# Selective scan: summing the states' products in channel layout instead of in token rows

## Reference, cut to what matters

```python
deltaA = jnp.exp(delta[..., None] * A)                     # A has 16 states for each of 512 channels
deltaBx = (delta * xs)[..., None] * B[:, :, None, :]
_, ys = jax.lax.associative_scan(combine, (deltaA, deltaBx), axis=1)   # h[t] = deltaA*h[t-1] + deltaBx
y = jnp.einsum('blcn,bln->blc', ys, C)                     # y = sum over n of h_n * C_n
out = (y + xs * D) * res
return x + out @ w_out
```

## Time and profile before

| | |
|---|---|
| runs | 2469.58, 2472.93, 2481.07 us; median 2472.93 |
| the profiled execution | 2463.2 us, its span 2461.4 us |
| granted TensorE clock, mean | 0.954 |
| first scan, last scan (start) | 69.2 us, 2339.4 us |
| instructions | 35873 |
| moved by DMA | 101.76 MB, mean 41 GB/s |

### The profile page before, as it was taken

How to read it: one execution, slowest core, us unless ns; L and a number is a source line. 1 busy time by engine, 2 the same in 40 slices (tenths; PEclk the granted TensorE clock), 3 DMA queues, 4 the chain that set the end, 5 groups by cost and what they waited for, 6 DMA issues and landing times.

```text
span 2461.4 us, 35873 instructions
## 1 busy us (share of the span) xinstructions
PE 2128.8 (86%) x9268; PEld 1287.6 (52%) x9268; DVE 2187.0 (89%) x2820; ACT 1843.2 (75%) x3897; POOL 1854.4 (75%) x1324
## 2 busy tenths in 40 slices
PE   5687789898998989899898988989898998988797
PEld 2355455464655546465554646555464655546454
DVE  1889999998999999998999989999999989999931
ACT  6566787868788786978778687887869788785644
POOL 3868697887879788786877868797887879787620
PEclk8797899999999999999999999999999999999999
DMA  6011110111102021110202011020211102011100
GB/s 136 27 39 47 31 44 23 64 32 53 36 20 63 23 66 31 54 35 25 60 23 61 32 56 36 14 69 23 62 31 57 35 16 68 22 54 33 35 1 17
DMA packets 83404, 101.76 MB, mean 41 GB/s; under 512 B 23480, under 2 KB 49872, under 8 KB 83168
## 3 DMA queue, kind: packets, MB, share of 16 engines
q1 hardware_dynamic: 83168, 99.06, 13.7%
HBM read 90.13 MB, written 8.91 MB: 40 GB/s over the span
## 4 chain that ended last, share of the span: by engine, by line
PE 31%; DVE 28%; issue 21%; ACT 10%; POOL 8%; DVEq 1%; ACTq 0%; DMA 0%; POOLq 0%
PE bank L798 16%; DVE h L1348 12%; DVE yT L1364 9%; PE stateT L971 6%; PE bank L950 5%; POOL bx L766 5%; ACT decay L1217 3%; DVE xs L1257 2%; PE bank L936 1%; DVE rows L1283 1%; PE bank L860 1%; ACT rows L1009 1%; DVE st_b L1244 1%; PE bank L952 1%; DVE cumT L1303 1%
## 5 line engine op out<-in xcount | busy, mean ns | idle before, releaser
L766 POOL TENSOR_TENSOR bx<-dx,B_rows 128x1024 f32<-128x1024 f32 x512 | 1204.1, 2364 | 267.7 <-DVE h L1348 265.1
L1348 DVE TENSOR_TENSOR_SCAN h<-decay,bx 128x512 f32<-128x512 f32 x1024 | 1242.5, 1214 | 77.0 <-ACT decay L1217 63.3
L1217 ACT ACTIVATE decay<-delta,decay_rate 128x512 f32<-128x512 f32 x1024 | 705.0, 693 | 305.8 <-DVE h L1348 301.4
L971 PE MATMUL stateT<-ident,h 128*128 128x128 f32 x4096 | 633.2, 286 | 195.6 <-DVE h L1348 104.6
L971 PEld LDWEIGHTS stateT<-ident,h 128*128 128x128 f32 x4096 | 482.2, 145 | 508.5 <-issue 257.1
L1364 DVE SCALAR_TENSOR_TENSOR yT<-stateT,C_tok,yT 128x512 f32<-128x512 f32 x960 | 701.6, 731 | 17.6 <-PE stateT L971 15.8
L798 PE MATMUL bank<-k_to_expert,cumT 128*128 128x512 f32 x512 | 252.9, 618 | 9.4 <-ACT dx L1120 8.8
L798 PE MATMUL bank<-q_to_expert,xnT 128*128 128x512 f32 x512 | 252.9, 619 | 5.2 <-DVE xs L1257 5.2
L798 PE MATMUL bank<-hT,w_in_sb 128*128 128x512 f32 x512 | 244.4, 602 | 4.1 <-DVE xs L1257 1.5
L1183 ACT ACTIVATE cum_sb<-bank,gate 128x64 f32<-128x64 f32 x1024 | 222.0, 324 | 28.0 <-PE bank L798 25.9
L950 PE MATMUL bank<-expert_to_out,prodT 128*128 128x256 f32 x1024 | 238.3, 381 | 0.5 <-ACT cum_sb L1183 0.5
(11 more groups left out here) (155 smaller groups left out, 2596.1 us busy)
## 6 DMA issues: line engine op xcount, KB each, us to landing
B_rows<-B_scratch SPq DMA_DIRECT2D x256, 256.0 KB, 3.3
x_front<-in_L_attn_x SPq DMA_DIRECT2D x16, 512.0 KB, 6.0
x_back<-in_L_attn_x SPq DMA_DIRECT2D x16, 512.0 KB, 6.6
out<-x_back SPq DMA_DIRECT2D x16, 512.0 KB, 3.4
w_in_sb<-in_L_attn_w_in SPq DMA_DIRECT2D x1, 1024.0 KB, 5.8
cum_sb<-in_L_ffn_V_fwd SPq DMA_DIRECT2D x2, 256.0 KB
prod<-in_L_ffn_W_inv_exp SPq DMA_DIRECT2D x2, 256.0 KB
xnT<-in_L_ffn_W_fwd SPq DMA_DIRECT2D x2, 256.0 KB
```

Of the source, the lines that this page charges most:

```text
L766: pool.tensor_tensor(bx[use % BX_RING][:, :, :], dx[q.parity][:, 2 * half:2 * half + 2, :], row, ALU.mult).then_inc(s_bx.step(f"{n},{half} ...
L971: last = pe.transpose(stateT[j % 2][:, c * P:(c + 1) * P], h[n % 2][:, c, j * P:(j + 1) * P], ident[:, :])
L1217: act.activation(decay[c % 2][:, :], delta[q.parity][:, c, :], ACT.Exp, scale=decay_rate[:, c, n:n + 1]).then_inc(s_exp.step(f"{n},{c}"), 1)
L1348: dve.tensor_tensor_scan(h[n % 2][:, c, :], decay[c % 2][:, :], bx[(2 * n + c // 2) % BX_RING][:, c % 2, :], 0.0, ALU.mult, ALU.add).then_ ...
```

## The change

The products of state and C stay in channel layout. The row of C for state n is spread over all partitions by one TensorE product with a column of the identity matrix (`C_all`, a PSUM bank). VectorE multiplies all four tiles of h by it in one instruction of 128x2048 into one of two buffers `weighted`. Three of its four tiles are added onto `xs` by a transfer that GpSimd issues and that adds at its destination; before that ScalarE has multiplied those three tiles of xs by D (`skip_task`). The fourth tile is summed over the states on TensorE in a PSUM bank `y_last` (product with the identity, accumulating), and VectorE adds it to `xs * D` once. There is one h buffer now. The transposes of h, of yT and of C, the sums L1364 and three of four `u` instructions are gone. The two residual sums become adding transfers too, `x_task` one instead of two halves. The whole TIMETABLE is written anew; of it only a few entries stand here.

```diff
 TIMETABLE = {
-    ("B", "u", "dve"): (264, 264, 264, 269),
+    ("B", "u", "dve"): (266,),
+    ("F", "skip", "act"): (120, 122, 127),
-    ("B", "gelu", "act"): (337,),
+    ("B", "gelu", "act"): (338,),
-    ("L", "cum", "act"): (357, 360, 368, 379, 391, 392, 408, 432),
+    ("L", "cum", "act"): (360, 367, 371, 378, 399, 402, 407, 437),
...
+ADDED = CT - 1
+WEIGHTED_AT, C_AT, ADDED_AT = 7, 1, 2
...
-        h = [sb(f"h{i}", P, CT, T) for i in range(2)]
-        yT = sb("yT", P, TB, DI)
+        h = sb("h", P, CT, T)
+        weighted = [sb(f"weighted{i}", P, CT, T) for i in range(2)]
...
-        stateT = [psum(f"stateT{i}") for i in range(2)]
+        C_all = psum("C_all")
+        y_last = psum("y_last")
```

GpSimd:

```diff
             def x_task(b, k, use):
 
-                half = slice(2 * k, 2 * k + 2)
-                pool.wait_ge(l_act.sem, l_act.done(b, f"t{2 * k + 1}"))
-                pool.tensor_tensor(x_back[b.parity][:, half, :], x_back[b.parity][:, half, :], o_rows[:, half, :], ALU.add).then_inc(l_pool.step(f"x{k}"), 1)
+                pool.wait_ge(l_act.sem, l_act.done(b, "t3"))
+                pool.sem_inc(passed["pool"], 1)
+                pool.dma_start(x_back[b.parity][:, :, :], o_rows[:, :, :], accum_op=ALU.add).then_inc(out_added, 16)
...
+            def add_product(batch, n):
+                pool.wait_ge(s_mul.sem, s_mul.done(batch, f"{n}"))
+                pool.sem_inc(passed["pool"], 1)
+                if n == 0:
+                    pool.wait_ge(f_act.sem, f_act.done(batch, f"sk{ADDED - 1}"))
+                    pool.sem_inc(passed["pool"], 1)
+                if n or batch.shift(-1).exists:
+                    pool.wait_ge(y_added, batch.count(16 * NS, 16 * n))
+                    pool.sem_inc(passed["pool"], 1)
+                pool.dma_start(flat(xs[batch.parity][:, 0:ADDED, :]), flat(weighted[n % 2][:, 0:ADDED, :]), accum_op=ALU.add).then_inc(y_added, 16)
+
             def scan_part(q, n, beat):
+                if beat == ADDED_AT:
+                    batch, done = (q, n - 2) if n >= 2 else (q.shift(-1), NS - 2 + n)
+                    if batch.exists:
+                        add_product(batch, done)
```

TensorE:

```diff
             def scan_part(q, slot, beat):
-                if beat % 2:
+                if beat != C_AT:
                     return
...
-                for c in range(CT):
-                    last = pe.transpose(stateT[j % 2][:, c * P:(c + 1) * P], h[n % 2][:, c, j * P:(j + 1) * P], ident[:, :])
-                last.then_inc(s_tr.step(f"{n},{j}"), 1)
+                if batch.exists:
+                    pe.wait_ge(s_mul.sem, s_mul.done(batch, f"{n}"))
+                if q.exists:
+                    if slot == 0:
+                        pe.sem_inc(passed["pe"], 1)
+                        pe.wait_ge(f_act.sem, f_act.done(q, "C"))
+                    rows_of_q = 64 + 32 * q.parity
+                    pick = ident[rows_of_q:rows_of_q + NS, rows_of_q + slot:rows_of_q + slot + 1].broadcast_to([NS, P])
+                    pe.matmul(C_all[:, :], pick, C_rows[q.parity], start=True, stop=True).then_inc(s_C.step(f"{slot}"), 1)
+                if batch.exists:
...
+                    pe.matmul(y_last[:, :], ident[:, :], weighted[n % 2][:, ADDED, :], start=(n == 0), stop=(n == NS - 1)).then_inc(s_sum.step(f"{n}"), 1)
```

ScalarE (and in `proj_task` one copy of C's 16 rows more, in place of the `Ct` copy) and VectorE:

```diff
+            def skip_task(b, c, use):
+                act.wait_ge(f_pool.sem, f_pool.done(b, f"dx{c}"))
...
+                act.activation(xs[b.parity][:, c, :], xs[b.parity][:, c, :], ACT.Copy, scale=skip_sb[:, c:c + 1]).then_inc(f_act.step(f"sk{c}"), 1)
...
                     if c == 0:
-                        free = q if n >= 2 else q.shift(-1)
+                        free, back = (q, n - 1) if n else (q.shift(-1), NS - 1)
                         if free.exists:
-                            dve.wait_ge(s_tr.sem, s_tr.done(free, f"{(n - 2) % NS},{TB - 1}"))
+                            dve.wait_ge(s_mul.sem, s_mul.done(free, f"{back}"))
...
+                if beat != WEIGHTED_AT or not q.exists:
                     return
...
+                if free.exists:
+                    dve.wait_ge(s_sum.sem, s_sum.done(free, f"{back}"))
+                    dve.wait_ge(y_added, free.count(16 * NS, 16 * (back + 1)))
+                dve.wait_ge(s_C.sem, s_C.done(q, f"{n}"))
+                dve.wait_ge(s_scan.sem, s_scan.done(q, f"{n},{CT - 1}"))
+                dve.tensor_tensor(weighted[n % 2][:, :, :], h[:, :, :], C_all[:, :].rearrange("p (o t) -> p o t", o=1).broadcast_to([P, CT, T]),
+                                  ALU.mult).then_inc(s_mul.step(f"{n}"), 1)
```

More of the change, by code:

```diff
@@ L288, in program @@
         projT = hT[0:NPROJ, 0, :]
-        C_tok = [sb(f"C_tok{i}", P, TB, NS) for i in range(2)]
         st_b, st_1 = (sb(f"st_{n}", P, TB, 6) for n in "b1")
@@ L600, in store @@
             def store(batch, k, use):
[L601 removed]
+                sp.wait_ge(out_added, batch.count(16, 16))
                 sp.sem_inc(passed["sp"], 1)
@@ L853, in dt_task @@
                 matmuls(use.bank[:, :], [(w_dt_sb[:, c * P:(c + 1) * P], projT[0:RANK, :])]).then_inc(f_pe.step(f"dt{c}"), 1)
-            def y_task(b, c, use):
-                if c == 0:
-                    pe.wait_ge(s_acc.sem, s_acc.done(b, f"{NS - 1},{TB - 1}"))
-                pe.wait_ge(use.sem, use.free_at)
-                for j in range(TB):
-                    last = pe.transpose(use.bank[:, j * P:(j + 1) * P], yT[:, j, c * P:(c + 1) * P], ident[:, :])
-                last.then_inc(b_pe.step(f"y{c}"), 1)
             def wo_task(b, k, use):
@@ L1366, in scan_part @@
-                ins.then_inc(s_acc.step(f"{n},{k}"), 1)
+                n = slot
+                free, back = (q, n - 2) if n >= 2 else (q.shift(-1), n - 2 + NS)
+                if free.exists:
[5 more added lines that the diff above has]
+                                  ALU.mult).then_inc(s_mul.step(f"{n}"), 1)
```

242 lines of the change are left out of this document (109 added, 133 removed), and 10 rows, old and new, of tables (FILLED_BY, TIMETABLE).

## The result

The changed kernel takes 2552.47 us, median of four runs (2550.27 to 2553.42), beside 2472.33 us for the kernel before: ratio 1.0317, 95% interval 1.029 to 1.0343. The prediction said 2455, 0.7% faster, in a range up to 2555. The sign was wrong; the time lies at the range's upper end, where the rival "GpSimd becomes the bound" stands.

A forecast was written before the change was run, and what follows sets the result against it. VectorE bounds the kernel, 136.5 us busy in 143.9 a batch. 131.9 + 6.8 + 2.3 + 1.3 = 142.3 us against 143.9 is -26 us, tail +8: 2455 us by the median; own range 2430 to 2480, with rivals 2385 to 2555.

The forecast's parts named there:

- GpSimd becomes the bound: Rival, chance 0.27: GpSimd's issue in front of the second bx makes the kernel slower, 2523 us at 1.8 us an issue.
- VectorE: 136.5 - 4.6 = 131.9 us a batch: VectorE's work: the wide product saves 2.7 us a batch, three u instructions fewer save 1.9.
- the hand-overs: VectorE between scans and product: a dependent instruction cannot overlap its predecessor, 0.11 us each, twice a state.
- the bound of 2.40 given for the product: VectorE's wide product: upper bound, four times the whole pitch, where 2.17 us was taken.
- GpSimd ... 131 us a batch ... VectorE's waits 2.3: GpSimd's queue: 116.0 - 4.9 + 19.8 us for 18 issues; VectorE's waits for bx and followers 2.3 instead of 0.8.
- The threshold g = 1.65 us: GpSimd's issue in front of the second bx: the time g per issue that decides whether GpSimd becomes the bound.
- ScalarE ... 6.8 us a batch: VectorE's waits for ScalarE's exps, as scans come in a burst and long tasks do not split: 6.8 instead of 3.9.
- TensorE falls to about 103 us: TensorE a batch: from 129.5, transposes out, two products a state at 0.47 us in.
- Rival 4: TensorE's clock falls as its slots empty: 129 us a batch at a mean of 0.8, 2479 us; chance 0.08.
- Landing 5 us, hidden: Adding transfers of 768 KB: land in 5 us, bounds 3.7 and 6.0, hidden behind the next state's scans.
- Tail +8: Behind the last scan: +0.5 for the last state's transfers, +3.2 for x1, +4 for the last x, in us.
- 2430 to 2480: Whole kernel: the forecast's own range in us, said to be half the distance to each term's bounds; chance 0.42.

The follow-up runs named there:

- e2: The changed kernel with GpSimd's dx moved right behind its w2, so that GpSimd stops for the delta sum at once: 2555.47 us, ratio 1.0364.
- e8: The changed kernel without the states' adding transfers and their waits, and with GpSimd's dx right behind w2: 2495.31 us, ratio 1.011.
- e16: The kernel before, plus only one small adding transfer issued by GpSimd per state (256 in all) that nobody reads: 2508.33 us, ratio 1.0156.
- e7: The changed kernel without the states' 16 adding transfers a batch, issue and waits; residual transfers stand: 2494.77 us, ratio 1.0122.
- e3: The changed kernel with the two residual sums made as additions on GpSimd again instead of adding transfers: 2545.47 us, ratio 1.0316.
- e18: The changed kernel without TensorE's sum and the skip of tile 3, the freed PSUM bank a third buffer for decay: 2534.84 us, ratio 1.0262.
- e9: The changed kernel with the TensorE product that spreads C's row made twice, 256 products more: 2707.03 us, ratio 1.0962.
- e4: The changed kernel with the adding transfer moving one tile (256 KB) instead of three; issue and waits stand: 2551.78 us, ratio 1.0333.
- e11: The changed kernel with the adding transfer issued at beat 6, behind the second bx, instead of beat 2: 2789.23 us, ratio 1.1302.
- e13: The changed kernel with all four tiles added by transfer (1 MB a state), no TensorE sum or u, a fourth skip: 2617.96 us, ratio 1.06.
- e12: The changed kernel with TensorE's sum of the fourth tile cut to 16 of 512 columns except at the last state: 2550.58 us, ratio 1.0328.

## Why the prediction was wrong, step by step

- **"VectorE: 136.5 - 4.6 = 131.9 us a batch" held as work, and failed as the busy time that it was said to be.** The figure counts the hand-overs, 16 x 0.22 = 3.5 us, which a profile shows as idle; as busy time it should have read 128.4. The stretch has 137.0, of which the hold is 8.2; the rest is 128.8. `u` went as said. A bare state costs 7.09 in place of 6.91: the product takes 2.29 us where 2.17 was reckoned, and stands 0.12 and 0.10 us off its neighbours. The slope of 1.02 ns was from sums with one input from PSUM; it was the right price within 5%, yet the saving was smaller than this 5%. That the saving came all the same is partly luck: other tasks fill many hand-overs, and of the idle 11.8 us only 2.1 are not in the list of waits. A gain that is a difference of two large terms should carry the error of both: by the bound of 2.40 given for the product, the state's saving is below nothing.
- **What no step had**: L1273 held by GpSimd's reads, 8.2 us a batch in the stretch. By the books this is the whole miss: work and hand-overs 130.9, listed waits 9.7 and the hold 8.2 make 148.8, against 131.9 and 10.4 of waits in the forecast's 142.3. The prediction asked what a fuller GpSimd does to those who wait for it, and not to those who share its way into SBUF. But e2 and e8 show that without the hold the time is the same, so this omission explains where the time is seen and not the result.
- **"GpSimd ... 131 us a batch ... VectorE's waits 2.3" was the step that failed most.** The issue was sized well, 0.9 us against 1.1, and GpSimd's busy time is 126.4 a batch (1466.83 / 11.6). VectorE's waits for bx even fell, to 4.0 us in all. What failed is the pricing: I priced GpSimd's load by who waits for bx, at 2.3 - 0.8 = 1.5 us a batch. e16 shows 39 us for the issues alone, and e7 57 us, 3.6 a batch. That alone turns the sign: 57 us in place of 24 would have made the forecast 2488. The loss comes up as the hold, or with the hold away as waits on other engines; the way there, through the other tasks in GpSimd's order, is argued. The threshold g = 1.65 us for this rival supposed that GpSimd costs nothing until it is full; the issues cost part of each microsecond long before (e3's sums, elsewhere in the order, did not).
- **"ScalarE ... 6.8 us a batch" held**, roughly: 8.2. The cause named, long tasks that don't split and the pieces of room, fits e18, where a third bank leaves 108 of 123 us; it is not shown.
- **"TensorE falls to about 103 us" failed.** It stays at 133 (1548.58 / 11.6). One group of the earlier trace rows reads x4 for two products, each of two instructions; I took it for four, as does the heading of these rows. A product is 1.05 us, not 0.47, so C and the sum put back all that the transposes took. e9 shows that this engine has no room for more. VectorE has no wait for TensorE in the stretch, where 1.3 us a batch were forecast; TensorE's lateness can reach it only through others. Rival 4 had the clock's sign right (0.92 in the stretch, 0.97 before), though TensorE was not emptied.
- **"Landing 5 us, hidden" held**: 6.0, the upper bound, and e4 shows it hidden. The estimate of 5.6 by the Trainium skill (Collectives: The Full Stack, on the reduce primitive) was nearer than the 5 taken. e11 and e13 show how near the edge it is.
- **"Tail +8" held**: +8.9.
- **The ranges.** "2430 to 2480" does not follow from its terms: half the distance to the bounds, added up, is -3.6 and +7.4 us a batch, so 2398 to 2573, and a gain of 18 us inside it was no sign to rely on. That 2552 lies within the stated 2385 to 2555 is luck: the upper end stood for an issue of 1.9 us that fills GpSimd, and the issue took 0.9 with GpSimd idle for 15% of the stretch.

Of the 80 us by the medians, the issues account for 57 in the changed kernel (39 where nothing else changed). Left over in e7 are 22 us, 9 of them the tail. The rest is 0.8 us a batch by the medians and 1.5 by the traces: exp waits of 8.9 us in place of 3.9 and a hold of 3.8, less what VectorE saved. That split is by subtraction. How much TensorE shares in it is open, since no run changed TensorE's work with the clock held. Untested is also the new timetable by itself: all tasks were placed anew together with the change, and no run has the old places.

## What to carry to other kernels

When four engines are each at 75 to 90% of a period and bound to each other by many short waits, price added work on any of them by a share of it (here 0.15 to 0.3 us for each issue of 0.9 us on GpSimd, 0.6 for each 1.05 of TensorE), not by nothing until it is full; and work taken off the busiest one at a third. The share depends on the place in the order: two sums of 2.36 us a batch in place of two issues cost nothing (e3). Ask also whose busy time is really a hold. Before counting on a saving, count the instructions of a profile's group against the source (x512 for 256 products), and put the error of each term beside the difference. An experiment that puts only the suspected cost into the kernel before (e16) says more than one that takes a wait away, since waits move.

## What the runs showed of the hardware

- A VectorE sum with both inputs in SBUF took 4.6 to 4.7 us, twice a batch, behind GpSimd's row of instructions that read SBUF, and 2.0 us with only 8 columns; it ended when GpSimd's queue stopped, and took 0.68 where that queue stopped at once (e2).
- An adding transfer costs GpSimd 0.9 to 1.0 us to issue whatever its bytes (906 ns for 768 KB, 980 for 256 KB, 1019 for 8 KB), 0.6 before the next instruction starts and 0.3 by which that one is longer. It landed in 3.4 us for 256 KB, 4.6 to 5.6 for 512, 6.0 for 768 and 7.5 for 1024.
- An fp32 product of 512 columns is two instructions of TensorE, 1.05 us (0.94 by the pitch of the earlier trace rows).
- Dependent neighbours on VectorE stood 0.10 to 0.12 us apart; independent ones overlap by 0.08 (1011.50 + 0.66 and 1012.08).
- TensorE with 496 columns fewer per state ran at a lower mean granted clock (0.871 against 0.899), and about half of the 199 us taken off came back in its other products. Its two levels are 1.2 and 2.4 GHz, and a mean between them is a share of time at each: of 60 slices of 1 us in e12 (1000 to 1060), 42 stand at 1.00, 15 at 0.50 and 3 between.
